# A two-layer graph network on one core: row sums of squares by sixteen short ScalarE squares in place of one ScalarE square and a VectorE sum

## The reference, cut to what matters

```python
def _layernorm(x, axis=-1, eps=1e-05):
    m = jnp.mean(x, axis=axis, keepdims=True)
    v = jnp.var(x, axis=axis, keepdims=True)
    return (x - m) / jnp.sqrt(v + eps)
...
    h = jnp.maximum(_layernorm(x, axis=-1), 0.0)
    x = x + _L0_gnn_ref(h, edge_index, ...)      # two GCN layers, 64 -> 128 -> 64, over the edges
    h = jnp.maximum(_layernorm(x, axis=-1), 0.0)
    x = x + _L1_gnn_ref(h, edge_attr_64, ...)    # relational attention over the edges, two 64 x 64 products
```

## Time and profile before

| | |
|---|---|
| median of 3 runs | 4698.17 us (4695.47 to 4700.88) |
| profiled execution | 4714.36 us, span 4712.6 us |
| granted TensorE clock, mean of the span | 0.61 of full speed |
| busy in the span: POOL, DVE, ACT, PE | 73%, 49%, 22%, 29% |

### The profile page before, as it was taken

One profiled execution on the slowest core, in us unless ns is written; L12 is line 12 of the kernel. 1 busy time (PEld: TensorE's weight loads), 2 busy tenths in 40 slices (PEclk: granted clock), 3 DMA queues, 4 the chain that ended last, 5 costly groups with the idle time before them and its releaser, 6 DMA issues.

```text
span 4712.6 us, 29671 instructions
## 1 busy us (share of the span) xinstructions
PE 1370.1 (29%) x7306; PEld 1093.9 (23%) x7306; DVE 2316.6 (49%) x3229; ACT 1013.3 (22%) x1595; POOL 3451.5 (73%) x3153
## 2 busy tenths in 40 slices
PE   2455468850134342000000000013346500333331
PEld 1344356640122221000000000012235400232231
DVE  6777777850366665888760010012222200666663
ACT  2333345530122221111110001012222200122220
POOL 7666667777788786777757777777747777588887
PEclk8666678875566666555555555555555655666666
DMA  5666766730123233555542222233433300111110
GB/s 173 214 210 209 220 207 206 213 120 1 47 81 93 82 92 94 189 184 191 203 138 63 77 75 71 73 106 120 123 120 94 91 24 1 32 54 56 58 54 27
DMA packets 375176, 528.24 MB, mean 112 GB/s; under 512 B 232608, under 2 KB 245002, under 8 KB 375014
## 3 DMA queue, kind: packets, MB, share of 16 engines
q1 hardware_dynamic: 268166, 426.25, 27.6%
q0 software_dynamic: 106848, 100.11, 8.7%
HBM read 265.55 MB, written 264.64 MB: 113 GB/s over the span
## 4 chain that ended last, share of the span: by engine, by line
POOL 58%; issue 19%; PE 7%; DVE 7%; DMA 7%; ACT 1%; SPq 1%; POOLq 1%; DVEq 0%; ACTq 0%
POOL arena L1147 28%; POOL result L1142 10%; POOL input_and_place_by_node L1142 9%; POOL slot_rows L1142 8%; POOL relf L1147 4%; DMA arena<-in_x 4%; DMA work<-slot_rows 2%; PE banks L1612 2%; PE banks L1510 2%; DVE arena L467 1%; PE banks L1502 1%; SPq L923 1%; DVE arena L453 1%; PE banks L1600 1%; DVE t_stat L458 1%
## 5 line engine op out<-in xcount | busy, mean ns | idle before, releaser
L1142 POOL DMA_INDIRECT result<-work,outi x392 | 501.5, 1279 | 164.2 <-issue 122.3
L1147 POOL DMA_INDIRECT work<-in_x,dsafe x392 | 416.1, 1062 | 222.2 <-issue 114.1
L1147 POOL DMA_INDIRECT arena<-input_and_place_by_node,src_i x392 | 477.0, 1217 | 119.5 <-issue 119.5
L1147 POOL DMA_INDIRECT arena<-g_by_node_and_edge,m_idx x392 | 446.2, 1138 | 121.2 <-issue 119.2
L1142 POOL DMA_INDIRECT input_and_place_by_node<-work x392 | 425.4, 1085 | 147.6 <-issue 128.9
L1142 POOL DMA_INDIRECT slot_rows<-work,dsafe x392 | 403.9, 1030 | 140.8 <-issue 119.2
L1147 POOL DMA_INDIRECT arena<-h_by_node_and_edge,m_idx x392 | 402.7, 1027 | 119.5 <-issue 119.5
L1147 POOL DMA_INDIRECT relf<-slot_scores,src_i x392 | 369.9, 944 | 159.3 <-issue 127.9
L1600 PE MATMUL banks<-ident,work 128*128 128x128 f32 x456 | 111.8, 394 | 881.4 <-DMA work<-slot_rows 880.7
L765 DVE TENSOR_TENSOR work<-work,ends 128x896 f32<-128x896 f32 x28 | 46.7, 1668 | 565.3 <-DMA work<-h_by_node_and_edge 558.5
L1600 PEld LDWEIGHTS banks<-ident,work 128*128 128x128 f32 x456 | 81.2, 205 | 897.8 <-issue 692.7
(11 more groups left out here) (287 smaller groups left out, 4908.1 us busy)
## 6 DMA issues: line engine op xcount, KB each, us to landing
arena<-in_x SPq DMA_DIRECT2D x96, 512.0 KB, 5.8
slot_rows<-work SPq DMA_DIRECT2D x48, 912.0 KB
work<-slot_rows SPq DMA_DIRECT2D x114, 384.0 KB, 3.3
input_and_place_by_node<-arena SPq DMA_DIRECT2D x49, 528.0 KB, 2.8
arena<-input_and_place_by_node SPq DMA_DIRECT2D x49, 512.0 KB, 6.8
g_by_node_and_edge<-arena SPq DMA_DIRECT2D x49, 512.0 KB, 2.8
h_by_node_and_edge<-arena SPq DMA_DIRECT2D x49, 512.0 KB, 3.0
arena<-x_of_destination SPq DMA_DIRECT2D x56, 448.0 KB, 4.4
```

The costliest lines, as they stand in the source:

```text
L1142: pool.indirect_dma_start(out=table[:, :], out_offset=bass.IndirectOffsetOnAxis(ap=idx, axis=0), in_=of, in_offset=None, bounds_check=boun ...
L1147: pool.indirect_dma_start(out=to, out_offset=None, in_=table[:, :], in_offset=bass.IndirectOffsetOnAxis(ap=idx, axis=0)).then_inc(signal, 16)
```

## The change

In both node passes the one square of 128 x 1024 becomes sixteen squares of 128 x 64, one for each of the block's 16 columns of rows, and each of them also gives its sum along the 64 features into one number per partition (`accum_out`). The two VectorE sums over the squares are gone. Semaphores, buffers and the order of the steps stay. The lines behind the edit have other numbers in the changed kernel (two less or one more than before).

```diff
             def t_variance(b):
                 st = t_stat[:, b % 2]
                 dve.wait_ge(T["square"], b + 1)
-                ot.do(v.tensor_reduce(st[:, 0, :], cols(tsq), AX.X, ALU.add))
                 ts(st[:, 2, :], st[:, 0, :], 1.0 / D, EPS, ALU.mult, ALU.add).then_inc(T["var"], 1)
...
             def q_variance(b):
                 st = q_stat[:, b % 2]
                 dve.wait_ge(Q["square"], b + 1)
-                oq.do(v.tensor_reduce(st[:, 0, :], cols(qsq), AX.X, ALU.add))
                 ts(st[:, 2, :], st[:, 0, :], 1.0 / D, EPS, ALU.mult, ALU.add).then_inc(Q["var"], 1)
...
                 if b < NB:
                     act.wait_ge(T["centered"], b + 1)
-                    activation(tsq, tx[:, b % 3], ACT.Square).then_inc(T["square"], 1)
+                    for c in range(CB):
+                        at = slice(c * D, (c + 1) * D)
+                        ins = activation(tsq[:, at], tx[:, b % 3, at], ACT.Square, accum_out=t_stat[:, b % 2, 0, c:c + 1])
+                    ins.then_inc(T["square"], 1)
...
             def q_square(b):
                 act.wait_ge(Q["centered"], b + 1)
-                activation(qsq, qxc, ACT.Square).then_inc(Q["square"], 1)
+                for c in range(CB):
+                    at = slice(c * D, (c + 1) * D)
+                    ins = activation(qsq[:, at], qxc[:, at], ACT.Square, accum_out=q_stat[:, b % 2, 0, c:c + 1])
+                ins.then_inc(Q["square"], 1)
```

## The result

The changed kernel takes 4789.38 us (median of 4 runs, 4784.84 to 4803.87), the kernel before beside it 4696.82 us (4 runs). The ratio is 1.0198 (95% interval 1.0181 to 1.0214): 92.6 us slower (85 to 100 by the interval). The forecast was slower, 4828 us, range 4762 to 4961.

What follows compares the result with a forecast made beforehand. A chain of waits through all engines, not a load, was taken to bound the interleaved node passes. Terms of 113, 2.6, 11.7 and 3 us summed to 130, added to the median of 4698.2: 4828 us, range 4762 to 4961.

Steps and rivals of the forecast that it cites:

- the loop: Interleaved passes: waits through SyncE, TensorE, ScalarE and VectorE, 27.2 us from load to load, two blocks of pass t, one of q.
- 2S - 3.6: Growth in us of each interleaved period, two runs of sixteen squares in a row; 5.4 us, 113 us over 21 periods.
- S: Time on ScalarE from the first of sixteen squares until it can go on: 4.5 us forecast, 0.96 before.
- forecast case: ScalarE's sixteen squares with reads take 3.5 to 5.7 us: 4762 to 4883 us, chance 0.62.
- the first blocks: Six blocks of pass t ahead of pass q, where variance waits for the squares: 11.7 us added.
- the first step of pass q: From the first square of pass q to VectorE's variance for the block behind: 9.2 us against 6.6, so 2.6 added.
- 3 us for POOL: Allowance for POOL's scatters running slower beside a longer pass q; at most 11 us, taken as 3.
- cheap-read rival: Accumulator read on ScalarE free or nearly so, S = 2.5 us: 4725 us, chance 0.11.
- the slack: VectorE's 201.3 us wait for POOL's first edge-pass gathers, to absorb up to 95 us from pass q running alone.
- The read without overlap: On ScalarE each accumulator read waits until its square has left the pipe, S up to 7.1 us: 4961 us, chance 0.20.
- The faster case: ScalarE hides sixteen squares within 1.8 us, only VectorE's vanished sum counts: 32 us faster, 4666 us, chance 0.03.
- The equal case: Pass t's delay is caught by another wait, so the time stays: chance 0.04.

Runs made afterwards that it cites:

- t_only: Kernel before with column squares and their sums in pass t alone, pass q as before: 4728.71 us against 4700.24 (ratio 1.0057).
- q_only: Kernel before with column squares and their sums in pass q alone, pass t as before: 4755.83 us (ratio 1.0116).
- split_keep_sum: Changed kernel without accumulator outputs: sixteen squares in both passes, VectorE's two sums kept: 4738.55 us (ratio 1.0069 to the kernel before).
- both_moves: Kernel before; ScalarE's root and square for even blocks between pass q's halves, pass q's square behind pass t's two steps: 4599.26 us (ratio 0.9773).
- the moved square: Pass q's square put behind pass t's two steps: on the changed kernel 4715.11 us, on the kernel before 4683.13, each against 4706.44 before.
- q_tail_only: Kernel before with sixteen squares and sums only in pass q's 27 blocks after pass t: 4702.13 us against 4700.24 (ratio 1.0005).

## Why the prediction was right, and where its size was off

**What bounds.** Right: the loss has arisen at the end of pass t, 88.7 us there and 92.6 in the median, and such a delay passes on about one for one. In the ten other kernels the first scatter moved by an amount within 9 us of the change of the median: 23 and 28 us in `t_only`, 57 and 56 in `q_only`, 44 and 38 in `split_keep_sum`, -104 and -107 in `both_moves`. That the profiled executions differ by 70.5 us only (4783.1 against 4712.6) lies in the 392 gathers for the edge pass, for which POOL was busy 477 us in the profiled execution before and 460 in the one after; the median before is 4697, below its profiled execution's 4714.

**What it removes and adds, on the loop.** Right in form: the two squares stand there in a row, the sum is gone, and the growth per period is 4.01 us where 2S - 3.6 with the measured S gives 4.06. The split by halves, the tail and the moved square each gave what the formula says within 16 us, and the moved square, a change of place alone, tells it from the load.

**The size of S.** Too high: 4.5 us forecast, 3.83 measured, inside the 3.5 to 5.7 of the forecast case. The term is the spacing of a square with its read, put at 0.28 us, measured 0.24. Its two parts were near: 0.145 for the square, where interpolation gave 0.155, and 0.095 for the read, where VectorE's row gave 0.11. The rest was a surcharge for ScalarE's longer shortest instruction. It was not needed: the read lasts 0.19 us, about as long as that instruction, but an instruction's length is not its spacing, since the next one starts some 0.09 us before it ends. The formula makes 28 us of it (21 x 2 x 0.67), and the first blocks and the first step of pass q 5 more (8 x 0.67). With the measured S the sum is therefore 97 us in place of 130. Without its 3 us for POOL it says 94 at the hand-over, where 88.7 were measured; the loads' landing, 0.3 us shorter per period, makes 6 us. So the period came out at 30.9 us, not 32.5, and the first scatter at 749 us, not 787. The 3 us for POOL did not show: its scatters took 553 us from first to last before and 552 after. The prediction's own test of the mechanism, 22 x (2S - 3.6), gives 89 us with the measured S. That it meets the 88.7 is in part luck: it leaves out some 8 us of the first blocks, which the shorter landings happened to offset.

The Trainium skill ("ScalarE: Activation LUTs", section "What ACT_TABLE_LOAD costs") gives, as an estimate worked out from its figures, 146 ns for the spacing of squares of 64 columns; `split_keep_sum` shows 0.146 us. Its rule for the spacing was better here than the interpolation. It prices no accumulator read, and by it alone the forecast would have been about that of the cheap-read rival, 4725 us, 64 us too low.

**The first blocks and pass q alone.** The first load of pass q came at 59.79 us against 52.88, 6.9 us later. The five blocks ahead of that load were forecast at 2.2 + 4 x 1.9 = 9.8 with the larger S; with the measured one the same terms give 6.4. Pass q alone was allowed up to 95 us, to be taken by the slack. That bound was right and far too wide: the stretch did not grow at all, in the changed kernel or in `q_tail_only`, and VectorE's wait at its end stayed at 204 us.

**The rivals.** The free read is refuted by the row of the read, 0.095 us each. The read without overlap likewise: both overlap. The faster case needed 0.113 us for square and read; it was 0.24. The equal case needed the loop to shorten its load by as much: it gave back 0.3 of 4.0 us.

What stays open: why the granted clock is at its upper level in some periods and not in others, and whether the change of the period moves that. One execution of each kernel, with 3 to 6 such periods of 20, does not tell.

## What to carry to other kernels

Before you trade one engine's operation for several on another, look in the chain of waits for what stands directly behind it in that engine's queue: here a square that nobody needed soon delayed a root that everybody waited for. Ask first whether the order in the queue can be changed; two moves in ScalarE's queue, without a change of the work, gave 107 us, where moving the sums onto ScalarE cost 93. And price a run of short instructions by the spacing of their starts, each accumulator output counted as an instruction of its own, not by their lengths.

## What the runs showed of the hardware

A ScalarE square of 128 x 64 with an accumulator output is an ACTIVATE of 0.24 us and an ACTIVATION_READ_ACCUMULATOR of 0.19 us, and the pair repeats at 0.24 us; without the output the same square repeats at 0.146 us. Sixteen with sums take 3.83 us, sixteen without 2.34, one of 1024 columns 0.96, each to the point where ScalarE can go on.
